# Twelve instead of eight of seventeen down projections in three reduced-precision passes, with four of the remainders formed on POOL

## What is computed

```python
scores = sigmoid(x @ gate_w.T)
_, inds = top_k(scores + expert_bias, 8)
combine = ...                                  # weights of the 8 chosen experts, 0 for the others
hg = einsum('bsd,eid->bsei', x, w_gate)
hu = einsum('bsd,eid->bsei', x, w_up)
h = silu(hg) * hu
ye = einsum('bsei,edi->bsed', h, w_down)
y = einsum('bsed,bse->bsd', ye, combine)
y = y + (silu(x @ shared_gate.T) * (x @ shared_up.T)) @ shared_down.T
x = layernorm(x + y)
```

## Time and profile before

| | |
|---|---|
| median of 3 runs | 718.38 us (716.48 to 720.23) |
| profiled execution, its own time | 717.01 us |
| its span in the trace | 715.3 us |
| PE busy | 678.9 us, 95% |
| DVE busy | 580.4 us, 81% |
| ACT busy | 448.0 us, 63% |
| POOL busy | 348.0 us, 49% |
| granted PE clock, mean over the span | 0.965 |

### The profile page before, as it was taken

The page is one execution under the profiler, slowest core; times in us unless marked ns, Lnnn a source line. Parts: engine busy times, 40 slices in busy tenths (PEclk is TensorE's granted clock), DMA queues, the critical chain, the costliest instruction groups (busy, mean ns, idle before and its releaser), DMA issues. The chain is left out here.

```text
span 715.3 us, 13700 instructions
## 1 busy us (share of the span) xinstructions
PE 678.9 (95%) x3558; PEld 373.8 (52%) x3558; DVE 580.4 (81%) x1149; ACT 448.0 (63%) x843; POOL 348.0 (49%) x373
## 2 busy tenths in 40 slices
PE   3799999999999999999998899999999999999995
PEld 1343333433334334343322777777777777777773
DVE  1888998999999999999972577887879797978655
ACT  2058787888879888798886454545454544545431
POOL 3033252433424243252333666668676776676673
PEclk8569999999999999999999999999999999999998
DMA  5833241422514224142102305060513314050601
GB/s 180 256 110 88 84 141 52 138 73 83 157 47 139 86 59 154 54 149 68 49 4 109 129 2 237 0 252 0 198 53 120 131 46 205 15 236 0 251 1 29
DMA packets 34279, 74.89 MB, mean 105 GB/s; under 512 B 4144, under 2 KB 13488, under 8 KB 30032
## 3 DMA queue, kind: packets, MB, share of 16 engines
q1 hardware_dynamic: 33440, 72.38, 29.2%
q0 software_dynamic: 816, 2.23, 1.1%
HBM read 58.61 MB, written 15.99 MB: 104 GB/s over the span
## 5 line engine op out<-in xcount | busy, mean ns | idle before, releaser
L762 ACT ACTIVATE probs<-ps_k 128x512 f32<-128x512 f32 x500 | 262.7, 606 | 52.2 <-PE ps_k L868 47.5
L805 DVE TENSOR_REDUCE maxima<-ps_bank 128x1 f32<-128x512 f32 x384 | 245.3, 682 | 27.4 <-PE ps_bank L861 22.3
L1113 POOL TENSOR_TENSOR hidden<-gated,weights 128x512 f32<-128x512 f32 x128 | 189.1, 1493 | 93.1 <-DVE gated L1213 79.5
L1152 ACT ACTIVATE silu<-ps_gate 128x512 f32<-128x512 f32 x136 | 80.7, 599 | 134.8 <-PE ps_gate L1257 134.6
L861 PE MATMUL ps_bank<-k_aug,q_aug 32*128 32x512 f32 x384 | 147.6, 510 | 11.9 <-DMA q_aug<-q_rows 8.3
L868 PE MATMUL ps_k<-q_aug,k_aug 32*128 32x512 f32 x500 | 154.2, 488 | 3.8 <-ACT probs L762 2.2
L881 PE MATMUL ps_ctx<-probs,v_ones 128*32 128x512 f32 x1024 | 139.6, 618 | 0.8 <-ACT probs L762 0.8
L868 PEld LDWEIGHTS ps_k<-q_aug,k_aug 32*128 32x128 f32 x500 | 63.9, 184 | 124.7 <-ACT probs L762 107.7
L1213 DVE TENSOR_TENSOR gated<-silu,ps_up 128x512 f32<-128x512 f32 x128 | 85.6, 683 | 45.3 <-PE ps_up L1257 26.9
L625 POOL TENSOR_TENSOR shift<-shift_raw,ones 16x128 fp32r<-16x128 f32 x31 | 13.8, 445 | 180.6 <-ACT shift_raw L730 180.6
L805 DVE TENSOR_REDUCE maxima<-ps_turned 128x1 f32<-128x512 f32 x128 | 87.1, 680 | 3.0 <-PE ps_bank L861 1.7
(11 more groups left out here) (127 smaller groups left out, 824.0 us busy)
## 6 DMA issues: line engine op xcount, KB each, us to landing
weights<-combine_rows SPq DMA_DIRECT2D x32, 1024.0 KB, 7.6
k_aug<-k_rows SPq DMA_DIRECT2D x32, 256.0 KB, 2.7
q_aug<-q_rows SPq DMA_DIRECT2D x32, 256.0 KB, 2.9
q_rows<-qk_high SPq DMA_DIRECT2D x16, 256.0 KB, 2.9
k_rows<-qk_high SPq DMA_DIRECT2D x16, 256.0 KB, 3.5
net_raw<-w_nets POOLq DMA_DIRECT2D x17, 128.0 KB, 2.4
xT_sb<-xT SPq DMA_DIRECT2D x8, 256.0 KB, 2.8
q_rows<-qk_low SPq DMA_DIRECT2D x8, 256.0 KB, 3.1
```

What stands on the lines that cost most here:

```text
L762: act.activation(probs[:, t, h, :], score_slot(i, last)[:], ACT.Exp, scale=ATT_SCALE).then_inc(exp_done, 1)
L805: dve.tensor_reduce(maxima[:, parity, TILES * h + t:TILES * h + t + 1], bank("q", (i - UNIT * AHEAD) % SCORES)[:], AX_X, ALU.max).then_inc ...
L1113: pool.tensor_tensor(hidden[:, s % RING, :], gated[:, s % UP_RING, :], r.weights[:, e, :], ALU.mult).then_inc(hidden_done, 1)
L1152: act.activation(silu[:, s % UP_RING, :], ps_gate[s % 2][:], ACT.Silu).then_inc(silu_done, 1)
```

## The change

Nets 1, 2, 3, 5, 6, 7, 9, 10, 11, 13, 14 and 15 are now done in three passes (before: the odd ones), so nets 2, 6, 10 and 14 are new; 0, 4, 8, 12 and 16 stay fp32. The remainders of the four new ones are formed by POOL, behind mul `n + 2`, with a semaphore of their own; those of the odd nets stay on DVE. ACT rounds four more nets in a batch. `split_downs` makes the parts of twelve nets in four pairs of instructions of three nets each, instead of eight nets in one pair. The ring of four `hidden_high` and `hidden_low` buffers stays.

```diff
-SPLITS = EXPERTS // 2
+SPLIT_NETS = [n for n in range(1, NETS) if n % 4]
+SPLITS = len(SPLIT_NETS)
...
             def split_downs():
-                odd = nets_down[:, 1:, :].rearrange("p (j two) d -> p j two d", two=2)[:, :, 0, :]
-                ones = r.ones[:, 0:P].unsqueeze(1).to_broadcast([P, SPLITS, P])
+                ones = r.ones[:, 0:P].unsqueeze(1).to_broadcast([P, 3, P])
                 pool.wait_ge(r.downs_loaded, DMA)
-                pool.tensor_tensor(downs_high[:], odd, ones, ALU.mult).then_inc(r.downs_high_made, 1)
-                pool.wait_ge(r.downs_high_made, 1)
-                pool.tensor_tensor(downs_low[:], odd, downs_high[:].bitcast(F32), ALU.subtract
-                                   ).then_inc(r.downs_split, 1)
+                for j in range(0, SPLITS, 3):
+                    n = SPLIT_NETS[j]
+                    whole, high, low = nets_down[:, n:n + 3, :], downs_high[:, j:j + 3, :], downs_low[:, j:j + 3, :]
+                    pool.tensor_tensor(high, whole, ones, ALU.mult).then_inc(r.downs_high_made, 1)
+                    pool.wait_ge(r.downs_high_made, j // 3 + 1)
+                    pool.tensor_tensor(low, whole, high.bitcast(F32), ALU.subtract).then_inc(r.downs_split, 1)
...
     def splits(s):
-        n = s - 2
-        return n > 0 and n % 2 == 1
+        return s - 2 in SPLIT_NETS
...
         @block.gpsimd
         def _(pool):
+            def split_hidden(b, n):
+                j = SPLIT_NETS.index(n)
+                pool.wait_ge(hidden_highs, SPLITS * b + j + 1)
+                pool.tensor_tensor(hidden_low[:, j % SPLIT_RING, :], hidden[:, n % RING, :],
+                                   hidden_high[:, j % SPLIT_RING, :].bitcast(F32), ALU.subtract
+                                   ).then_inc(hidden_split_pool, 1)
...
                         pool.tensor_tensor(hidden[:, s % RING, :], gated[:, s % UP_RING, :], r.weights[:, e, :],
                                            ALU.mult).then_inc(hidden_done, 1)
+                    if splits(s) and (s - 2) % 4 == 2:
+                        split_hidden(b, s - 2)
...
-                    if splits(s):
+                    if splits(s) and (s - 2) % 4 != 2:
                         split_hidden(b, s - 2)
...
-                elif n % 2 == 1:
-                    j = n // 2
+                elif n in SPLIT_NETS:
+                    j = SPLIT_NETS.index(n)
...
-                    pe.wait_ge(hidden_split, SPLITS * b + j + 1)
+                    pe.wait_ge(hidden_split_pool if n % 4 == 2 else hidden_split, lows(b, n))
```

More of the change, by code:

```diff
@@ L1027, in splits, with lows @@
     def splits(s):
-        n = s - 2
-        return n > 0 and n % 2 == 1
+        return s - 2 in SPLIT_NETS
+    def lows(b, n):
+        mine = [m for m in SPLIT_NETS if (m % 4 == 2) == (n % 4 == 2)]
+        return len(mine) * b + mine.index(n) + 1
     with ExitStack() as ctx:
@@ L1063, in feed_forward @@
         hidden_split = sem("hidden_split")
+        hidden_split_pool = sem("hidden_split_pool")
         down_done = sem("down_done")
@@ L1136, in round_hidden @@
             def round_hidden(b, n, first):
-                j = n // 2
+                j = SPLIT_NETS.index(n)
                 act.wait_ge(hidden_done, EXPERTS * b + n)
                 if j >= SPLIT_RING:
-                    act.wait_ge(down_done, NETS * b + n - 2 * SPLIT_RING + 1)
+                    act.wait_ge(down_done, NETS * b + SPLIT_NETS[j - SPLIT_RING] + 1)
                 elif not first:
-                    act.wait_ge(down_done, NETS * (b - 1) + n + 2 * (SPLITS - SPLIT_RING) + 1)
+                    act.wait_ge(down_done, NETS * (b - 1) + SPLIT_NETS[j - SPLIT_RING] + 1)
                 act.copy(hidden_high[:, j % SPLIT_RING, :], hidden[:, n % RING, :]).then_inc(hidden_highs, 1)
@@ L1319, in _ @@
             pe.wait_ge(r.downs_loaded, DMA)
-            pe.wait_ge(r.downs_split, 1)
+            pe.wait_ge(r.downs_split, SPLITS // 3)
             turn_context(pe, c, ident, 2 * BATCHES - 1, 1, c.ps_turned)
```

## The result

The changed kernel takes 759.51 us (median of 4 runs, 754.56 to 762.60), the kernel before in the same measurement 717.43 us (4 runs): a ratio of 1.0576, 95% interval 1.0519 to 1.0632 (a ratio is worked out over the runs of a measurement and can differ a little from the quotient of the two medians). That is 42 us more, where 26 were forecast, and above the range of 731 to 754. The profiled execution took 758.88 us, with a span of 757.2 against 715.3.

The account below looks back on a forecast made before the run. PE was taken to bound the feed-forward stage. Batches 1 to 6 at 3.35 us each (20.1), batch 0 (4.1) and batch 7 (2.0) summed to 26.2 us on 717.01, so 743 us; range 731 to 754.

Parts of the forecast that it names:

- the saving of 0.66 a batch: PE's downs: three passes instead of one fp32 down save 0.165 us a net, four nets in a batch.
- ACT's roundings: Four more roundings on ACT in front of a silu, put at nothing; 0.58 us once a batch if one delayed it.
- the ring of four: Four buffers now hold 5.3 nets instead of 8; net 6's round waits for down 1, put at nothing.
- What I cost at nothing: `split_downs`: End of attention: eight instructions, 8.0 us instead of 4.7, covered by ACT's last context copy with margin 0.2.
- not what it says: Rival: late passes start slowly or the clock falls in stalls, 5 to 10 us a batch, 780 us or more; chance 0.02.
- The terms of a batch: Latenesses at nets 2, 6, 10 and 14 sum to 4.0 us, less 0.66 saving: a batch 3.35 us longer.
- The upper bound of a remainder, 1.49: POOL's 128x512 remainder takes 1.28 to 1.49 us, the upper from muls beside a busy DVE (two in 2.98).
- Feedback: In a batch: earlier stalls shrink later ones, net 10 from 1.45 to 1.2, net 14 to 0.75, net 2 to 1.0.
- blocking: Rival: each POOL remainder costs one DVE instruction 0.73 us, two on the path, 1.5 a batch more, 753 us; chance 0.10.
- The end: Batch 7: stalls for net 14 of batch 6, net 6 and the last remainder (1.7), less savings 0.8: 2.0 us.
- In time: Rival: PE never waits for remainders and only the saving is left, 711.7 us; chance 0.03.
- absorbed: Rival: engines catch up in each stall, only nets 6 and 10 are late, 1.6 a batch, 732 us; chance 0.13.

Follow-up runs that it names:

- the load alone: Changed kernel with PE's downs of nets 2, 6, 10 and 14 back in fp32, ACT and POOL still doing the new work: 728.87 us, ratio 1.0165.
- alone: Changed kernel with weights split early and only one of the four nets new: net 6 725.44 us, net 14 732.37 us, net 2 730.68 us.

## Why the prediction was wrong

The direction and the main mechanism were right: PE waits for POOL at the four nets, most at net 2 of batch 0, and the saving of 0.66 a batch drowns in it. Rightly put at nothing were ACT's roundings and the ring of four, within 0.2 a batch. The size, 26 instead of 42 us, failed at these steps: the start of the stage (4.9, forecast 0), batch 0 (3.7 too little), the six batches (6.1 too little, 3.5 by the terms of a batch and 2.6 by the clock) and the end (1.0).

**"What I cost at nothing: `split_downs`", margin 0.2.** Eight instructions of 1.00 to 1.01 us, 8.2 in all, were sized rightly, but ends were compared: POOL's end with the end of ACT's copy. PE starts 1.92 us after POOL's end and 0.46 after the copy's, so the real margin was -1.4 even with the cover of 8.25 us of the earlier trace rows. The 1.5 between are the DRAIN that ends POOL's part of the stage, and the prediction didn't look at it. That cover was itself partly luck: the granted clock was 0.66 from 385 to 390 there. In the changed kernel it was 1.00 from 385 to 396, and the cover 6.86 us. Together 2.8 us of wait. Behind it the first nine passes come 0.43 us apart, and down 0 is 2.3 us later against the start of the stage; 0.8 of it comes back at net 1, whose wait of 0.86 nearly goes. The other 2.1 of the 4.9 are not the change's: the attention stage ended that much later.

**The clock, as "not what it says", 0.02.** I priced one large case, a clock that stays down over 10 us of each batch, and took the quiet 1.00 of today's small waits as proof for new ones. What happens is in between: 8 to 14 passes at 1.2 GHz behind some waits. Batch 0 is 2.8 late at net 2 (a wait of 2.50), near the forecast of 2.6, and has 3.1 us of slow passes and slow `gate` behind it that weren't forecast; with the 1.5 net at the stage start and 0.2 at net 2 that is 4.8 more than forecast, less 1.0 for net 6, which wasn't late there: about the gap between 4.1 and 7.8. Three of the six batches have such a stretch and last 0.8 to 1.0 us more, 2.6 in all.

**The terms of a batch.** Undisturbed it costs 3.9 to 4.0 us and not 3.35. The last column does the prediction's own sum again, for a net by itself, with the two corrections named below:

| lateness, us | forecast | changed kernel | alone | sum done again |
|---|---|---|---|---|
| net 2 | 1.0 | 1.44 | 1.33 | 1.31 |
| net 6 | 1.05 | 1.21 | 1.20 | 1.20 |
| net 10 | 1.2 | 1.09 | not run | 1.55 |
| net 14 | 0.75 | 0.23 | 1.74 | 1.75 |
| step 0 | 0 | 0.68 | 0 | |

- Net 2 is 0.44 over its forecast, most of it an error of reading. "Mul 4 ends at about 563.89, a third of 4.23": the row stood for three muls, and they aren't alike. The first lies beside DVE's `hidden_low`, the next two take 1.27. Asked for by themselves, muls 4, 8 and 12 of the kernel before are these:

```profile
562.48 1.75 POOL L1113 TENSOR_TENSOR hidden<-gated,weights 128x512 f32<-128x512 f32 x1
...
571.93 1.29 POOL L1113 TENSOR_TENSOR hidden<-gated,weights 128x512 f32<-128x512 f32 x1 [0.92 <-DVE gated L1213]
...
580.92 1.30 POOL L1113 TENSOR_TENSOR hidden<-gated,weights 128x512 f32<-128x512 f32 x1 [2.04 <-DVE gated L1213]
```

So mul 4 ended at 564.23, 0.34 later than read, and muls 8 and 12 at 573.22 and 582.22, 0.2 sooner than the half of their rows.

- The upper bound of a remainder, 1.49, was the mean of two unlike muls, 1.29 and 1.73. Beside a DVE instruction that reads two tiles from SBUF the remainder takes 1.72 (nets 6, 10, 14), else 1.26 (net 2). At nets 6 and 10 the two errors, the mul read as too late and the remainder taken as too short, nearly cancel; that the band of net 6 held was partly luck. With the single ends, these two lengths and 0.04 by which a POOL instruction is recorded as starting before the one ahead ends, the prediction's way of reading gives the last column, within 0.02 of all three nets that ran alone.
- Feedback was there and stronger than forecast: net 14 is 1.74 late alone and 0.23 late behind the others. But the shift of POOL against DVE that comes with it has a price of its own. `x1T_low` now begins together with mul 16 and lasts until after its end, and PE waits 0.68 for it at step 0, two passes ahead of `down(14)`, which is one reason why so little is left there. The two together are 0.91 against 0.75. PE is marked as waiting for a remainder 20 times in the kernel and not 25 to 30 times, mostly because so little is left at net 14.

**The rival "blocking".** It had a chance of 0.10 and 1.5 us a batch. Its mechanism is real: `result` 3.04 instead of 2.07, and `picked` 1.18 instead of 0.23, beside a remainder; `x1T_low` 1.82 instead of 0.94 where it starts with a mul, which it used to meet in that mul's last 0.39 us. Of its price 0.68 a batch reached PE in the changed kernel; the rest is hidden behind the waits for POOL, and shows only when they are gone (1.2 a batch with the load alone, 1.0 of it from remainder 10). (The Trainium skill, SBUF — State Buffer, section "Who interferes with whom", has a DVE instruction of two SBUF inputs and a GpSimd instruction that reads SBUF block each other fully; 0.23 to 1.18 for `picked` agrees. `result`, which reads one large tile and two columns, is slowed as well.)

**The end, 3.0 instead of 2.0.** The last remainder makes PE wait 2.09 us, a lateness of 2.4 where 1.7 was forecast: that remainder takes 1.71 us beside DVE. Net 6 there is 0.7 late instead of 0.3.

**"In time", "absorbed".** Neither happened. Moving the remainder one mul earlier shows how near "in time" was: then no wait for POOL is left in the loop, and with net 10 left out a batch is shorter than before.

Not settled: why the attention stage ends up to 10 us apart from one trace to the next, and what decides that a wait of 1.05 us is followed by the lower clock in two batches and not in four, nor behind one of 2.51 us.

## What to carry to other kernels

A saving on the engine that bounds is worth what the slowest of its new suppliers allows: before splitting more work, write down for each place when the supplier ends and when the engine will ask, and put the supplier's instruction one slot earlier if it fits. Ungroup rows before taking an end time from them, and compare starts of the waiting engine, not ends of its suppliers: at the join of the two stages the two releasers differed by 1.5 us. Where another stage lies ahead and its end moves by several us from run to run, compare the stage and its batches, not the whole time. A wait of 1 us on PE can cost 1.5 us more in clock, so a sum of waits is a lower bound.

## What the runs showed of the hardware

- At the join of the two stages PE starts 0.42 to 0.44 us behind the last engine's DRAIN in all fourteen traces. POOL's DRAIN ends 1.48 us after the recorded end of its last subtraction, ACT's 0.04 after its copy. In the loop, where PE waits for the remainder's semaphore alone, there is no such time: the third pass of net 2 is recorded at 533.49, just after the remainder has ended at 533.44.
- POOL's 128x512 subtraction takes 1.26 to 1.30 us beside a DVE that is idle or reads PSUM, and 1.7 us beside one that reads two tiles from SBUF, and DVE instructions beside it become longer by up to the rest of the remainder.
- The granted clock fell to 0.50 behind a wait of 1.05 us in front of eight 16-column matmuls in two of six batches. It did not behind 2.51 us at the same place in batch 0 of the same kernel, nor behind waits of 1.5 us in front of full passes.
